# Attention and routed experts on one core: raw-row beginning with centred weights, and the expert stage in front of slot 30

## The reference, cut to what matters

```python
xn = _layernorm(x, axis=-1)            # x: 8 x 512 x 128, f32
x = x + attn(xn, w_attn, w_proj, decay_raw) + ffn(xn, W1, W2, Wr)

# attn: 16 heads of 8 columns, causal
scores = q @ k.T / sqrt(8) + causal + logw      # logw = -log1p(decay * log1p(distance))
y = softmax(scores) @ v
return y @ w_proj

# ffn: 8 experts, 128 -> 512 -> 128, the best 2 of each token
probs = softmax(xn @ Wr.T); vals, idx = top_k(probs, 2)
out = sum over the two picks of (vals / vals.sum()) * (silu(xn @ W1[e].T) @ W2[e].T)
```

## Time and profile before

| | us |
|---|---|
| median of 3 runs | 526.27 |
| lowest and highest | 525.38, 529.73 |
| the profiled execution, its own time | 527.81 |
| span of the profiled execution | 526.0 |
| mean granted clock of PE | 0.974 |

### The profile page before, as it was taken

How to read it: one execution, slowest core, us unless ns; L and a number is a source line. 1 busy time by engine, 2 the same in 40 slices (tenths; PEclk the granted TensorE clock), 3 DMA queues, 4 the chain that set the end, 5 groups by cost and what they waited for, 6 DMA issues and landing times.

```text
span 526.0 us, 13373 instructions
## 1 busy us (share of the span) xinstructions
PE 481.0 (91%) x4316; PEld 349.8 (66%) x4316; DVE 358.6 (68%) x1406; ACT 333.8 (63%) x600; POOL 338.3 (64%) x566
## 2 busy tenths in 40 slices
PE   7667999999999999999999999999999999999920
PEld 6545565555565565565665665666999999999910
DVE  7596897988898888888888888971333333333326
ACT  3578878778878878878878878876232333333300
POOL 3874455547888888876888888970454555555524
PEclk9988999999999999999999999999999999999975
DMA  6566591570460460460460461454476776657349
GB/s 180 171 232 206 154 226 45 159 210 17 134 185 27 134 185 27 135 180 9 136 185 25 137 185 35 128 156 136 122 208 191 208 227 205 206 172 229 116 171 318
DMA packets 71826, 80.38 MB, mean 153 GB/s; under 512 B 8638, under 2 KB 52672, under 8 KB 71760
## 3 DMA queue, kind: packets, MB, share of 16 engines
q1 hardware_dynamic: 67440, 71.06, 46.7%
q0 software_dynamic: 4320, 8.47, 4.5%
HBM read 48.11 MB, written 31.84 MB: 152 GB/s over the span
## 4 chain that ended last, share of the span: by engine, by line
PE 75%; DVE 14%; POOL 3%; ACT 2%; DMA 2%; issue 2%; SPq 0%; DVEq 0%; POOLq 0%; ACTq 0%
PE psT L1291 25%; PE psO L1309 13%; PE ps L1336 12%; PE psT L1363 12%; DVE scores L1121 7%; PE ps L1266 7%; PE psM L1250 2%; POOL xn_all L734 2%; DVE x_all L535 2%; PE ps L1327 1%; PE psM L1320 1%; POOL rstd L727 1%; DMA probs<-picked_dram 1%; DVE x_all L1156 1%; ACT probs L884 1%
## 5 line engine op out<-in xcount | busy, mean ns | idle before, releaser
L1121 DVE CUSTOM_DVE_ANT_0 scores<-ps,wdist 128x256 f32<-128x256 f32 (+3 forms) x512 | 217.3, 485 | 27.7 <-PE ps L1266 27.0
L765 POOL TENSOR_SCALAR scores<-scores,row_max 128x256 f32<-128x256 f32 (+2 forms) x384 | 177.8, 478 | 59.6 <-DVE row_max L1121 58.7
L884 ACT ACTIVATE probs<-psT 128x512 f32<-128x512 f32 x320 | 173.9, 597 | 53.8 <-PE psT L1291 52.6
L1291 PE MATMUL psT<-ident,scores 128*128 128x128 f32 x1280 | 176.4, 281 | 2.9 <-ACT probs L884 2.9
L1291 PEld LDWEIGHTS psT<-ident,scores 128*128 128x128 f32 x1280 | 137.9, 141 | 60.4 <-issue 45.4
L783 POOL DMA_INDIRECT picked_dram<-scores,row_ring x71 | 69.8, 983 | 80.7 <-DVE scores L1173 79.3
L893 ACT ACTIVATE scores<-ps 128x512 f32<-128x512 f32 x71 | 42.4, 597 | 94.6 <-PE ps L1336 94.6
L1309 PE MATMUL psO<-probs,values 128*32 128x512 f32 (+3 forms) x1024 | 88.4, 441 | 0.0
L846 ACT ACTIVATE scores<-scores,row_max 128x512 f32<-128x512 f32 x128 | 85.7, 728 | 0.0
L1336 PE MATMUL ps<-scores,wdist 128*128 128x128 f32 x568 | 75.3, 276 | 0.8 <-DVE scores L1161 0.8
L1363 PE MATMUL psT<-wdist,scores 128*128 x568 | 75.5, 276 | 0.1
(11 more groups left out here) (140 smaller groups left out, 277.3 us busy)
## 6 DMA issues: line engine op xcount, KB each, us to landing
wdist<-w1t SPq DMA_DIRECT2D x71, 256.0 KB, 3.4
k_rows<-k_dram SPq DMA_DIRECT2D x64, 96.0 KB, 2.9
q_rows<-q_dram SPq DMA_DIRECT2D x64, 96.0 KB, 2.6
row_ring<-rows_dram SPq DMA_DIRECT2D x71, 65.0 KB, 2.9
probs<-picked_dram SPq DMA_DIRECT2D x8, 512.0 KB, 6.6
rows_dram<-row_ring SPq DMA_DIRECT2D x7, 585.0 KB, 5.5
k_dram<-k_parts SPq DMA_DIRECT2D x7, 384.0 KB, 2.4
q_dram<-q_parts SPq DMA_DIRECT2D x7, 384.0 KB, 2.6
```

Source lines behind the costliest of these rows:

```text
L765: last = nc.gpsimd.tensor_scalar(part, part, -1.0, row_max[:, r, tile, quad:quad + 1], ALU.mult, ALU.add)
L884: nc.scalar.activation(probs[:, at.ring(2), w, :], psT[:, w % 2], ACT.Exp, scale=-1.0).then_inc(exp_ready, 1)
L1121: last = nc.vector.tensor_tensor_reduce(out=scores[:, r, u, col:col + n], in0=bank[:, col:col + n], in1=wdist[:, at.g * QUADS + quad, SEQ ...
L1291: last = nc.tensor.transpose(psT[:, w % 2, place * P:(place + 1) * P], scores[:, at.ring(2), u, col + key * P:col + (key + 1) * P], ident[:])
```

## The change

**Beginning.** Only batch 0 is normalised before it is turned. Batches 1 to 7 are turned as raw rows of x. All weights that multiply normalised rows (keys, queries, values, router) are first multiplied on PE by the centring matrix (identity minus 1/128, built by POOL) and copied back by ACT; the router's weights come with `w_attn` in one load. The factor 1/std is applied later: to values by four ACT copies with a scale per batch (L971 of the changed kernel), to logits on POOL, to the turned rows by one DVE product per batch (`XN`, L1105) with a tile of 1/std that PE turns (`RT`), SP stores (`RO`) and loads back spread over 128 partitions (`RB`). All `VL` steps but the last stand in the prologue now, with three PSUM bank pairs. POOL normalises the rows of batches 1 to 7, which the experts need, in slots 1 to 7, four tiles a slot (`NR`). In slot 0 POOL subtracts all ten units (`GROUPS_BY_POOL`). In slot 1 `P1` stands behind the first turns of group 0.

**Sends.** 3, 3, 3, 4, 3, 3, 3, 4, 3, 3 tiles a slot: picks one in slots 8 to 17, picks two in 18 to 27.

**Experts.** All 71 expert slots stand at the start of slot 30, before `P1` of group 30. W2 lies in `xn_all`, free once the rows are sent; SP's `WL` in slot 29 loads it, then the first rows and four W1 tiles, `WL` in slot 30 four more.

**End.** The picked rows are loaded right behind the expert stage (into `wdist` heads 0 to 7 and `xn_all`). `PA` adds batch 0 at the end of slot 30, 1 at the end of slot 31 and the others at the end of slot 32 (POOL batches 0 to 3, DVE 4 to 7); slots 33 to 35 then hold the last attention product, the projection and its addition, and batch 7 is stored last.

Places of the program where instructions move:

The diff, cut to its core:

```diff
-DVE_BATCHES, POOL_BATCHES = (0, 1, 3, 4, 6, 7), (2, 5)
+DVE_BATCHES, POOL_BATCHES = (4, 5, 6, 7), (0, 1, 2, 3)
...
-EARLY = {0: (("VL", 12), ("LN", 4), ("LN", 5)),
...
+EARLY = {0: {0: (("LN", 10), ("LN", 11)),
+             1: (("VL", 28),) + tuple(("LN", h) for h in range(12, 16)),
+             2: (("CZ", 1),) + tuple(("LC", b * GROUPS) for b in range(6)),
+             3: (("XN", 4),),
+             4: (("V0", 0), ("RS", 3), ("LC", 24), ("LC", 28), ("CZ", 2)) + tuple(
...
+         1: {2: (("RT", 1),), 3: (("RO", 1),), 4: (("CZ", 3),)}}
+FIRST_ROWS_SLOT, ROW_TILES = 1, 4
+SENDS = (3, 3, 3, 4, 3, 3, 3, 4, 3, 3)
...
+GROUPS_BY_POOL = 1
...
+EXPERT_SLOT = NGROUP - 2
+SUMS = {EXPERT_SLOT: (0,), EXPERT_SLOT + 1: (1,), EXPERT_SLOT + 2: (2, 3, 4, 5, 6, 7)}
...
+    if n == EXPERT_SLOT:
+        steps += [("WL", 0, 2), ("MI", 0), ("MU", 0, 0)]
+        for s in range(SLOTS):
+            steps.append(("MD", 0, s))
+            if s + 2 < SLOTS:
+                steps.append(("MU", 0, s + 1))
+        steps.append(("PL", 0))
+    if n == EXPERT_SLOT - 1:
+        steps += [("WL", 0, 0), ("WL", 0, 1)]
...
+    steps.extend(("PA", 0, b) for b in SUMS.get(n, ()))
...
+                nc.gpsimd.tensor_scalar(centre, ident[:], 1.0, -1.0 / C, ALU.mult, ALU.add).then_inc(centre_ready, 1)
...
+                def centre_weights(at):
+
+                    pe.wait_ge(centre_ready, 1)
+                    pe.wait_ge(w_loaded, 16)
+                    mm(ps1[:, 0, 0:3 * C + EXPERTS], centre, w_qkv[:], start=True, stop=True).then_inc(centred_full, 1)
+
+                def rstd_turn(at):
+
+                    n = at.c
+                    pe.wait_ge(rstd_ready, 4 if n else 2)
+                    pe.wait_ge(vo_free, BATCH if n else 2)
...
+                def rows_step(at, first, end):
+
+                    for t in range(first, end):
+                        nc.gpsimd.tensor_scalar(xn_all[:, t, 3:], x_all[:, t, :], mean[:, t:t + 1], rstd[:, t:t + 1],
+                                                ALU.subtract, ALU.mult).then_inc(rows_normal, 1)
...
+                    v.tensor_tensor(xt[:, at.parity, :], xt[:, at.parity, :], yt[:], ALU.mult).then_inc(xt_scaled, 1)
...
+                    for t in range(TILES):
+                        tile = at.batches(TILES, t)
+                        last = nc.scalar.activation(value_cols[:, at.parity, t, :, 0:HD],
+                                                    v_back[:, t, 0:C].rearrange("p (h d) -> p h d", d=HD),
+                                                    ACT.Copy, scale=rstd[:, tile:tile + 1])
...
+                    if part == 0:
+                        sp.wait_ge(rows_sent, 16 * TOPK * NTILE)
+                        for dst, src in w2_parts:
+                            sp.dma_start(dst, src).then_inc(w2_dma, 16)
+                        for s in range(RING):
+                            load_rows(s)
+                        return
+                    if part == 1:
                         sp.wait_ge(slot_table, 6)
...
+                    sp.wait_ge(p1_free, (EXPERT_SLOT - 2 + part) * UNITS)
+                    for s in range((part - 1) * RING // 2, part * RING // 2):
+                        load_w1(s)
+
+                def picked_load(at):
+                    wait_all_sent(sp)
+                    for b in (0, 1, 4, 5, 2, 3, 6, 7):
...
+                for b in (0, 1, 4, 5, 6, 2, 3, 7):
```

More of the change, by code:

```diff
@@ L110 @@
 ACT_UNITS = (0, 1, 6, 7)
-POOL_UNITS = tuple(u for u in range(UNITS) if u not in ACT_UNITS)
-FILLS = 8
+GROUPS_BY_POOL = 1
+FILLS = 7
 PICKS_STEP, GAP_STEP = 12, 13
@@ L124, in score_place, with act_units, pool_units, units_done @@
     return 2 * i + strip, {3: 0, 2: 0, 0: 384, 1: pair * 256}[tile]
+def act_units(c):
+    return ACT_UNITS if c >= GROUPS_BY_POOL else ()
+def pool_units(c):
+    return tuple(u for u in range(UNITS) if u not in act_units(c))
+def units_done(units, c, ready):
+    return sum(len(units(k)) for k in range(c)) + sum(u < ready for u in units(c))
 def probs_place(tile, quad):
@@ L1245, in step @@
                             pe.wait_ge(xt_copied, 1)
[L1246 to L1247 removed]
+                        if kind == "KA" and at.c > 0:
+                            pe.wait_ge(xt_scaled, at.batches(1))
+                        if kind == "KA" and at.c == GROUPS:
+                            pe.wait_ge(vm_free, BATCH)
                         if at.c == 0:
```

340 lines of the change are left out of this document (206 added, 134 removed), and 22 rows, old and new, of tables (EARLY, PROLOGUE).

## The result

| | before | after |
|---|---|---|
| median, us (runs) | 526.55 (4) | 511.83 (4) |
| lowest and highest | 525.38, 529.73 | 511.43, 513.18 |
| profiled execution, own time | 527.81 | 511.92 |
| its span | 526.0 | 510.0 |

The change makes the kernel faster: the ratio is 0.972, with a 95% interval of 0.967 to 0.976. The forecast was 504.4 with a range of 498.5 to 511.0. The gain of 22 us that it gave turned out to be 14.7, and the time lies 0.8 us above the range.

A forecast was written before the change was run, and what follows sets the result against it. PE work was taken to bound steady slots and expert stage, so only 45 us without it could shrink. Start -6.0, slots +0.5, expert stage 137 and the end gave span 504.1, plus 1.8 minus 1.5: 504.4 us, range 498.5 to 511.

The forecast's parts named there:

- The start: From kernel start to slot 2's first scores: slot 2 begins at 47 to 48 instead of 53.55, 6.0 us gained.
- the first scores: Start: first scores made at 28 (26.5 to 30), 3 us later than before, behind seven value-and-router steps.
- POOL's ten units and its normalising: Slot 0 subtractions all on POOL; 28 normalisations in slots 1 to 7, 3.2 us a slot, costed at nothing.
- rival 4: Expert stage: PE, idle at the seam, runs on at 1.2 GHz; ends slower or about even; chance 0.04.
- rival 1: Start gives nothing back, with first scores at 28 or later and PE at lower clock: 510.4 us; chance 0.12.
- On DVE a product of 128x512 per batch ... falls beside 1.6 us idle a slot: Steady slots: the per-batch token product, 0.69 us, fits DVE's idle time and adds nothing.
- four sends a slot: Steady slots, four of them: one more send, 0.96 + 0.30 us, fits POOL's idle 1.8; nothing, at worst 4 x 1.3.
- DVE adds four batches in 8.6 ... from 486, ending at 495: End: DVE's additions of picked rows finish just before the last attention product; a pair 2 us late would show one for one.
- The last line of the prediction: Listed signs of being wrong, among them DVE still adding picked rows when the last attention product ends.
- projection 1.06: End: projection behind the last attention product takes 1.06 us, within a serial piece of 4.3 us.
- It stands 1.6 us. ... I keep 137.: Entry of the expert stage: PE waits 1.6 us for ACT, yet 71 expert slots still take 137 us.
- From span to median: After the span of 504.1: add 1.8 us for the run's own time, subtract 1.5 for the median, giving 504.4.

The follow-up runs named there:

- the kernel with four repairs: Kernel after with token product earlier in its slot, later wait for sends, reordered expert-stage entry, picked rows split five to three with POOL's last batch last: 510.86 us.

## Why the prediction failed

**Where it held.** That both ends held the time without PE work was right: the gain is all there. That in between only PE work counts was not, in a few of them (below). The start gave 7.5 us for 6.0; I had put the first scores at 28, and they were made at 24.76, as early as before, although seven value-and-router steps stand ahead of them. The first exponential was at 37.10 for 38.4. So this term came out better than forecast because a cost in it, 3 us later first scores, was not there; that hid a part of what the other terms lost. (The mask and six small logit instructions at 0.374 are seven, 2.6 us, where the sum has 2.3.) POOL's ten units and its normalising cost nothing that shows in slots 2 to 7 beyond 0.4 us. The table load let the next activation start at once at both seams (1.28 us from 332.22 and from 470.43, the next activations at 333.52 and 471.72). The granted clock was 1.00 all through the stage, so rival 4 did not come, and rival 1 did not either: the start gave more than forecast, not nothing.

**"On DVE a product of 128x512 per batch ... falls beside 1.6 us idle a slot".** This is the step that failed most: it put the product at nothing. The price, 0.69, was taken from an addition with one input in PSUM. The product has both in SBUF, and beside POOL's back-to-back run it took 2.9 us, twice; that alone cost 2.3 us (509.49 and 509.83 us, for 511.83, in the two runs that take it away, by different means). I asked whether the engine had room, and not what it shares. That four sends a slot cost nothing was wrong with it: they cost PE nothing by themselves, but they put POOL's run where the product was. In all, slots 2 to 29 took 3.6 us more than before where I allowed 0.5: 2.3 for the products, 0.9 in slots 18 and 19, where the wait for the sends stands (0.6 of it went when the wait was moved), 0.4 in slots 2 to 7.

The Trainium skill (SBUF — State Buffer, SBUF: two separate sides) says that the one thing the engines contend for is a port pair that VectorE and GpSimd share, held by one instruction for its whole length, also against a VectorE instruction with two SBUF inputs. By that rule, with the subtractions' 0.59 us from the trace, an estimate is 0.69 plus the rest of one subtraction, 1.3 us at most. The trace agrees in kind, but the wait was 2.2 us: it outlasted several subtractions.

**"DVE adds four batches in 8.6 ... from 486, ending at 495".** Both numbers failed. The additions stand behind slot 31's scores and output step on DVE and began at 490.34. And the 8.61 us in the earlier trace rows were a mixture: eight additions with POOL beside them for about half of the time. The trace of before has it, in that line's durations (ns, min/median/max) and in its first four additions, which had no POOL beside them:

```profile
509.96 2.87 DVE L535 TENSOR_TENSOR x_all<-x_all,probs 128x512 f32<-128x512 f32 x4 [7.00 <-DMA probs<-picked_dram]
...
L535 DVE TENSOR_TENSOR x_all<-x_all,probs x12: 691/692/1635, 510.0 to 521.7; 128x512 f32<-128x512 f32 x12
```

Three of the eight took 1.63 us each there. With POOL adding nearly throughout, eight took 11.64. The late 1.8 us showed one for one, as that paragraph said it would. The last line of the prediction named this sign; it should have been a term. With nothing beside them they take 0.72 us each.

**"projection 1.06".** It took 2.05 us in this execution: PE had stood 4.25 us, and the granted clock of this stretch was 0.5 to 0.6. That is 1.0 us, and it differs from kernel to kernel (below).

**"It stands 1.6 us. ... I keep 137."** The wait at the entry was as sized (1.08 + 0.37 = 1.45), but it was not added: the figure from before held the attention product just where PE would have stood. With 0.51 us for ACT later on, that is the 1.9. Two chains meet within 0.3 us at the first down product (the first product with W2), PE's own with its waits for DVE and the weights, and ACT's with the table load: shortening PE's alone gave nothing (the product came 4.21 us behind the entry for 4.22), shortening both brought it 1.2 us forward, of which the stage kept 0.4.

**From span to median.** I subtracted 1.5 us because the profiled run of before lay that much above the median. Each run's time is 1.7 to 2.4 us above its own span, and the profiled execution after was an ordinary one. The stretches that the sum kept from before had no such excess: the slots without a change took the same in both executions (9.14, 9.98, 10.02 and 10.33 us), and the expert stage was not shorter after. Of what was kept, at most the last store, 0.8 us longer before, can have held a part of it. This alone is 1.5 us of the 7.4, nearly twice what was missing to the range.

What stays open: 0.5 us in slots 30 and 31 beyond the table load, why the last store took 0.8 us less than before, and 3.3 us at the end of the kernel with four repairs, which no engine and no transfer shows.

## What to carry to other kernels

When an instruction is moved to an engine with room, look at where its operands lie and at what DVE or POOL does in the same microseconds: a DVE instruction like this product, with two SBUF inputs, belongs where POOL issues DMAs or idles, or takes one input from PSUM. A duration is worth what stood beside it when it was measured, so the price of a group that overlapped a neighbour for part of its run is no price for a full overlap. At a seam where several engines arrive together, list all chains with their times before costing the removal of one.

## What was unexpected in the hardware

**A held DVE instruction waits for more than one POOL instruction.** POOL's twelve subtractions run as 5.5 us without a gap. A product that arrived 2.78 us into such a run took 2.91; 2.79 into it, 2.90; 3.10 into it, 2.60; in each case until near the run's end, past the instruction running and about four more of 0.36 to 0.58 us. One that arrived 3.52 into it took 0.69, and there POOL's next subtraction took 1.00 us for 0.58; those 3.9 to 4.1 into it took 0.72 to 0.98. So between 3.10 and 3.52 us into the run it changes who waits. The additions, longer on both sides, took turns instead: 1.65 us each on DVE, 1.60 on POOL, for 0.69 and 1.28 alone. What decides was not tried. DVE's scores, with one input in PSUM, were never stretched beside POOL (128x512: 0.68 to 0.69 us, 128 of them).

**PE's clock after a wait.** After some 4.25 us of standing, the projection at the end took 2.04 or 2.05 us in five kernels, 1.74 in two and 1.13 or 1.15 in two; after 3.3 and 3.4 us, 1.13 in both; after 2.6 us, 1.67 in one and 1.13 in another. So the length of the wait alone does not tell the clock, what does is not shown, and this term is anything from 0 to 1 us in a forecast of this end.
